# The last mixer step's output handed to the routing front's rounds, and the front's order changed on three engines

## The chip, the cores and the metric

One Trainium2 chip, one of its cores. The metric is the device time of one execution of the whole program, in microseconds (us), of which three were taken for the kernel before.

## What is computed

A block with adaptive layer norm on 8 sequences of 512 tokens and 128 channels: four Mamba-2 layers (`ga` scales what comes out), and then a mixture of experts with one shared expert and 8 routed ones, of which each token takes its best two.

```
h = layernorm(x) * (1 + ca) + sa
for l in range(4):
    h = h + mamba2_layer(rmsnorm(h) * block_norm_w[l], ...)
    # in it: y = rmsnorm(y * silu(z)) * gw; return y @ W_out
x = x + ga * (rmsnorm(h) * final_norm_w)
h = layernorm(x) * (1 + cb) + sb
n = rmsnorm(h) * norm_weight
shared = relu(n @ sw1 + sb1) @ sw2 + sb2
probs = sigmoid(n @ router_w.T); w, idx = normalised top 2 of 8
x = x + gb * (shared + sum of w * expert[idx](n))
```

## The kernel before

Activations lie transposed: 128 channels on the partitions, the 512 tokens of one sequence (a *batch*, n = 0 to 7) in the free dimension. All five engines run hand-ordered lists of instructions with semaphores between them; nothing is scheduled by a tool. There are four stages.

1. *Input.* Load, layer norm, transposes.
2. *Mixer.* 32 steps of one layer and one batch, in a software pipeline of depth three: `body(k)` (L414 and on for TensorE, with a body of its own for each engine) does part A of step k, part B of step k-1 and part C of step k-2. Part C is the end of a layer: `project_out` (two matmuls with W_out, L493 and L494), `square_mean` of the gated output y2 (L479), on ScalarE `square_y`, `log_y`, `root_y` (L1044, L1050, L1055: log and exponential give the reciprocal root), on VectorE `scale_out` (L1484), on GpSimd the sum of the two squares (L1775) and the residual `add_to_h` (L1837). So k = 32 has parts B and C, and k = 33 has part C alone, that of batch 7 in layer 4. Into k = 32 and 33 the first pieces of the front for batch 0 and batch 1 are woven.
3. *Front.* For each batch: square, mean, root of h (`square_h`, `square_mean_of_h`, `root_h`), `add_mamba` (x = x + ga * rmsnorm(h), L1335 and L1338), `mean` and `centre` (L430, L1343), `square_x`, `variance`, `root_x` (L437), `modulate` (L1349, L1351), `square_m`, `square_mean_of_m`, `root_m` (L441, L947, L950), `scale` (L1357), which gives the router's and the experts' input nT. Then `halve` (nT as a sum of two fp32r halves, on ScalarE L955 and on VectorE L1362), `logits` (L446), `exp_logits` (L960), `probability` (L1376), `compare`, `ranks`, `choose` (L1384 to L1401: which two experts), `routing_weight` (L1407 to L1412), `positions` (prefix sums by matmul, L733), `slot` (L1419 to L1424: the row numbers for the scatter). The shared expert goes along: `shared_up(t)` (three matmuls each, L689 to L691, t = 0 to 3), `shared_relu(t)` (L1173), `halves(t)` (L1610, L1612), `shared_down(t)` (L700 to L703), `shared_result` (L1182), `add_shared` (L1618), `turn_base` and `keep_base` (L724, L1195). `turn_tokens` and `put_tokens` (L713, L1190) bring the tokens into rows, and GpSimd scatters them with eight indirect DMAs per batch (L1910) into the experts' slots, after `slot` of that batch.
4. *Experts.* 23 tiles of 512 slots, then the gather and the output.

The order of stage 3 is a function `front(i)` on TensorE, ScalarE and VectorE, called for i = -3 to 10 (`FRONT` is 3); in one round i the pieces belong to batches i-1 to i+3, and a condition drops those outside 0 to 7. The position of a line in `front(i)` is the position in the engine's queue. Before its rounds each of ScalarE and VectorE waits for the whole mixer:

```
steps(dve, body)
dve.wait_ge(hup, NB + STEPS)
```

(`hup` counts the residual sums), followed on VectorE by three set-up operations for the routing.

## Time and profile before

| | us |
|---|---|
| median of three executions | 1090.94 (1088.0 to 1091.41) |
| the profiled execution | 1089.98 |
| its span, first to last instruction | 1088.1 |
| TensorE busy in the span | 948.3 (87%) |
| VectorE busy | 959.5 (88%) |
| ScalarE busy | 846.6 (78%) |
| GpSimd busy | 777.4 (71%) |
| mean granted TensorE clock, share of full speed | 0.961 |

Busy shares are means over four stages. In the trace the mixer's steady part ends near 722 us, its last two bodies reach to about 762, the front's rounds to about 880, and the experts follow from 890. A row of the order of time reads: start, duration, engine, line, operation, output and inputs; in square brackets how long the engine sat idle before it, and what ended that.

### The profile page before, as it was taken

Reading aid. Unit: us, or ns where it says so; the run is one execution under the profiler, and the core shown is the slowest. Engines: PE = TensorE matmul, PEld = TensorE weight load, DVE = VectorE, ACT = ScalarE, POOL = GpSimd, SP = SyncE. Lnnn points to the kernel's source line nnn. Section 1 sums busy time; section 2 is a strip of 40 time slices with the busy share of each in tenths; the row PEclk is TensorE's granted clock in tenths of the full one; section 3 lists DMA queues with packets and bytes.
Section 4 is the critical chain, followed back from the end, with each engine's and each line's share of the span. In section 5 each row is a group of like instructions: output and inputs, shape, how many; then the busy total and the mean of one; then the engine's idle time right before and its main releaser. Section 6 shows DMA issues by size and latency. Waiting matters only on the chain.

```text
span 1088.1 us, 20653 instructions
## 1 busy us (share of the span) xinstructions
PE 948.3 (87%) x6072; PEld 543.3 (50%) x6072; DVE 959.5 (88%) x1769; ACT 846.6 (78%) x1604; POOL 777.4 (71%) x942
## 2 busy tenths in 40 slices
PE   5799999999999999999999999985888759999970
PEld 4344554454445544544554445443455537777750
DVE  6799999999999999999999999975888948888855
ACT  4699999899999998999899989974777625555530
POOL 1289989998998999888877886873355643666660
PEclk9799999999999999999999999998899969999995
DMA  5010232224222322100000000000011136776628
GB/s 151 17 27 13 73 140 71 71 80 152 72 71 85 128 76 86 64 3 3 4 10 2 4 4 4 4 2 1 20 35 35 40 116 190 233 229 224 226 89 231
DMA packets 57422, 83.93 MB, mean 77 GB/s; under 512 B 17562, under 2 KB 37664, under 8 KB 57312
## 3 DMA queue, kind: packets, MB, share of 16 engines
q1 hardware_dynamic: 52320, 74.13, 21.3%
q0 software_dynamic: 4992, 8.48, 2.3%
q8 instruction: 51, 0.84, 0.3%
q14 instruction: 59, 0.48, 0.1%
HBM read 44.99 MB, written 37.83 MB: 76 GB/s over the span
## 4 chain that ended last, share of the span: by engine, by line
PE 28%; ACT 22%; POOL 21%; issue 17%; DVE 8%; DMA 2%; SPq 1%; POOLq 1%; DVEq 0%; ACTq 0%
ACT E L976 3%; POOL dtx L1788 3%; POOL own L1820 3%; PE bank L468 3%; ACT xbc L1081 3%; PE bank L689 2%; POOL yt L1842 2%; PE bank L546 2%; POOL xw L1795 2%; PE bank L703 2%; PE bank L701 2%; PE bank L700 2%; ACT L1070 2%; POOL y L1846 2%; PE bank L690 2%
## 5 line engine op out<-in xcount | busy, mean ns | idle before, releaser
L1449 DVE SCALAR_TENSOR_TENSOR cv<-bank,PAR,cv 128x511 f32<-128x511 f32 (+2 forms) x384 | 276.5, 740 | 6.1 <-ACT cv L988 2.0
L976 ACT ACTIVATE E<-bank 128x512 f32<-128x512 f32 x256 | 144.5, 603 | 44.7 <-PE bank L532 40.1
L1465 DVE SCALAR_TENSOR_TENSOR M<-E,bank 128x512 f32<-128x512 f32 x256 | 170.2, 676 | 1.4 <-ACT E L976 0.4
L1917 POOL DMA_INDIRECT RS<-y,XR x92 | 99.5, 1082 | 78.1 <-DVE y L1697 53.6
L468 PE MATMUL bank<-hn,WA 128*128 128x512 f32 x256 | 142.5, 640 | 3.5 <-DVE cv L1449 3.5
L1842 POOL TENSOR_TENSOR yt<-yt,ti 128x384 f32<-128x384 f32 x64 | 64.1, 1002 | 74.4 <-DVE ti L1522 74.4
L1910 POOL DMA_INDIRECT XS<-stage,IDX x64 | 68.5, 1071 | 56.5 <-DVE run L1424 39.2
L1173 ACT ACTIVATE hr<-bank,W1B 128x512 f32<-128x512 f32 x92 | 63.5, 690 | 56.7 <-PE bank L691 48.9
L1612 DVE TENSOR_TENSOR hL<-hr,hH 128x512 fp32r<-128x512 f32 x124 | 86.9, 701 | 4.3
L1788 POOL TENSOR_TENSOR dtx<-xtok,DTW 128x256 f32<-128x256 f32 x128 | 79.8, 623 | 12.0 <-ACT xtok L996 8.1
L1846 POOL TENSOR_TENSOR y<-yt,zs 128x512 f32<-128x512 f32 x64 | 82.2, 1284 | 5.0
L546 PEld LDWEIGHTS bank<-M,dtx 128*32 128x32 f32 x2048 | 50.9, 109 | 60.5 <-DVE M L1465 32.1
L546 PE MATMUL bank<-M,dtx 128*32 128x128 f32 x2048 | 75.9, 277 | 5.4 <-DVE o_sb L1484 5.4
L1820 POOL TENSOR_TENSOR own<-p,selb 128x512 bf16<-128x512 bf16 x64 | 78.6, 1248 | 0.2 <-PE bank L532 0.2
L1610 DVE CAST hH<-hr 128x512 fp32r<-128x512 f32 x124 | 54.0, 435 | 26.1 <-issue 11.7
L1081 ACT ACTIVATE xbc<-cv 128x512 f32<-128x512 f32 x128 | 73.7, 632 | 0.0
L675 PE MATMUL bank<-hn,WA 128*128 128x512 f32 x128 | 67.5, 649 | 0.0
L1795 POOL TENSOR_TENSOR xw<-xtok,DTW 128x256 f32<-128x256 f32 x96 | 62.5, 651 | 0.0
L510 PEld LDWEIGHTS bank<-CST,xbc 128*128 128x128 f32 x384 | 43.4, 141 | 37.7 <-ACT u L1006 20.3
L996 ACT ACTIVATE xtok<-bank 128x384 f32<-128x384 f32 x128 | 58.1, 481 | 2.5
L510 PE MATMUL bank<-CST,xbc 128*128 128x128 f32 x384 | 54.2, 277 | 5.4 <-ACT u L1006 4.8
L602 PEld LDWEIGHTS bank<-xbc,S 128*128 128x128 f32 x384 | 46.9, 191 | 19.1 <-DVE S L1508 13.8
(239 smaller groups left out, 2586.2 us busy)
## 6 DMA issues: line engine op xcount, KB each, us to landing
XS<-PADT SPq DMA_DIRECT2D x32, 520.0 KB, 4.8
W1B<-WD SPq DMA_DIRECT2D x23, 514.0 KB
W2B<-WD SPq DMA_DIRECT2D x23, 512.5 KB
WD<-WS SPq DMA_DIRECT2D x16, 512.0 KB, 2.9
XR<-XS SPq DMA_DIRECT2D x23, 260.0 KB
RW<-w_in SPq DMA_DIRECT2D x18, 256.0 KB, 4.9
xin<-x_in SPq DMA_DIRECT2D x4, 512.0 KB, 8.5
PC<-p SPq DMA_DIRECT2D x128, 6.0 KB
```

Source lines behind the costliest of these rows:

```text
L468: mm(bank[t % 2][:, :], WA[t][:, :], hn[k % 2][:, :], start=True, stop=True).then_inc(pj_mm, 1)
L510: ins = nc.tensor.transpose(bank[TURN_BANK[c]][:, n * P:(n + 1) * P], conv_rows(t, odd + 1, c * CH, CH), ident)
L546: ins = mm(bank[6 + hh // 4][q:q + 32, c * CH:(c + 1) * CH], dtx[c][:, hh * HD:(hh + 1) * HD], M[2 * (hh // 4) + c % 2][:, (hh % 4) * CH:( ...
L976: f(E[i % 2][:, :], bank[2 + i % 2][:, :], ACT.Exp).then_inc(e_a, 1)
L1081: f(conv_rows(t, odd), cv[t][:, :], ACT.Silu).then_inc(silu_a, 1)
L1449: stt(out=cv[t][:, s:L], in0=src[:, 0:L - s], scalar=PAR[:, bass.ds(cw + 3 - s, 1)], in1=cv[t][:, s:L], op0=ALU.mult, op1=ALU.add).then_in ...
L1465: stt(out=M[i % 4][:, :].rearrange("p (n t) -> p n t", n=4), in0=E[i % 2][:, :].rearrange("p (n t) -> p n t", n=4), scalar=1.0, in1=bank[5 ...
L1612: tt(hL[t][:, :], hr[t][:, :], hH[t][:, :].bitcast(F32), ALU.subtract).then_inc(hl_v, 1)
L1788: tt(dtx[c][:, :].rearrange("p (h d) -> p h d", h=NH), xtok[c][:, 0:DI].rearrange("p (h d) -> p h d", h=NH), DTW[:, 32 * c:32 * c + NH].un ...
L1820: tt(own[:, g * 512:(g + 1) * 512].rearrange("p (h t) -> p h t", h=4), p2[:, :].unsqueeze(1).to_broadcast([P, 4, CH]), selb[:, g * 512:(g ...
L1846: tt(y2[t][:, :], yt[t][:, :], zs[:, bass.ds((j % 2) * 2 * L + t * L, L)], ALU.mult).then_inc(fin_p, 1)
L1917: nc.gpsimd.indirect_dma_start(RS[:, :], bass.IndirectOffsetOnAxis(ap=XR[i % XD][:, (c + 1) * ROW - 1:(c + 1) * ROW].bitcast(I32), axis=0) ...
```

## The change

- `body(33)` is gone on TensorE, ScalarE and VectorE (`steps` ends one k earlier). GpSimd's and SyncE's own loops stay as they are, with k = 33.
- Its work becomes items of the front: TensorE's `last_project_out` and `last_square_mean` in round -3 (now on banks 3 and 4), ScalarE's `last_square_y(0)`, `last_square_y(1)`, `last_log_y` and `last_root_y` in round -2, VectorE's `last_scale_out` in round -3.
- The pieces for batch 1 that were woven into k = 33 come from the rounds: conditions such as `2 <= i + 2` become `1 <= i + 2`.
- The waits for the whole mixer go; narrower ones guard the banks. The three set-up operations move into `choose(0)`.
- The order within `front(i)` is another one on all three engines.

```diff
@@ -227,7 +227,7 @@
 
         def steps(eng, body):
 
-            for k in range(STEPS + 2):
+            for k in range(STEPS + 1):
                 body(k, k % 2, A=k < STEPS, B=1 <= k <= STEPS, C=k >= 2, N=k < STEPS - 1)
...
                 wait(pe, n_v, n + 1)
                 if n == 0:
-                    pe.wait_ge(hup, NB + STEPS)
+                    wait(pe, fin_v, 4 * STEPS)
+                    wait(pe, o_v, STEPS - 1)
...
+            def last_project_out():
+
+                wait(pe, wos_a, 2 * NL)
+                wait(pe, fin_p, 4 * STEPS)
+                wait(pe, fin_v, 4 * STEPS)
+                mm(bank[3][:, :], WO[:, 0:DM], y2[0][:, :], start=True, stop=False)
+                mm(bank[3][:, :], WO[:, DM:2 * DM], y2[1][:, :], start=False, stop=True).then_inc(out_mm, 1)
+
+            def last_square_mean():
+
+                wait(pe, sum_p, STEPS)
+                wait(pe, s_v, 5 * STEPS)
+                wait(pe, e2_a, 2 * STEPS)
+                mm(bank[4][:, :], mean256[:, :], sqy[0][:, :], start=True, stop=True).then_inc(ss_mm, 1)
...
             def front(i):
 
+                if 1 <= i + 1 < NB:
+                    variance(i + 1)
                 if 0 <= i - 1 < NB:
                     turn_base(i - 1)
                 if 0 <= i < NB:
-                    shared_up(i, 0)
-                if 2 <= i + 2 < NB:
-                    mean(i + 2)
-                if 0 <= i < NB:
-                    shared_up(i, 1)
+                    shared_up(i, 2)
                 if 0 <= i < NB:
                     positions(i)
                 if 1 <= i + 1 < NB:
                     square_mean_of_m(i + 1)
                 if 0 <= i < NB:
+                    shared_up(i, 3)
+                if 1 <= i + 2 < NB:
+                    mean(i + 2)
+                if 0 <= i < NB:
                     shared_down(i, 0)
-                if 0 <= i < NB:
-                    shared_up(i, 2)
-                if 0 <= i < NB:
-                    shared_up(i, 3)
+                if i == -3:
+                    last_project_out()
                 if 1 <= i + 1 < NB:
                     logits(i + 1)
-                if 2 <= i + 3 < NB:
-                    square_mean_of_h(i + 3)
                 if 0 <= i + 1 < NB:
                     turn_tokens(i + 1)
                 if 0 <= i < NB:
                     shared_down(i, 1)
+                if 0 <= i + 1 < NB:
+                    shared_up(i + 1, 0)
                 if 0 <= i < NB:
                     shared_down(i, 2)
                 if 0 <= i < NB:
                     shared_down(i, 3)
-                if 1 <= i + 2 < NB:
-                    variance(i + 2)
+                if i == -3:
+                    last_square_mean()
+                if 0 <= i + 1 < NB:
+                    shared_up(i + 1, 1)
+                if 1 <= i + 3 < NB:
+                    square_mean_of_h(i + 3)
...
+            def last_square_y(t):
+
+                wait(act, fin_p, 4 * (STEPS - 1) + 2 + 2 * t)
+                wait(act, ss_mm, STEPS - 1)
+                f(sqy[t][:, :], y2[t][:, :], ACT.Square).then_inc(sq_a, 1)
+
+            def last_log_y():
+
+                wait(act, ss_mm, STEPS)
+                wait(act, o_v, STEPS - 1)
+                f(lnY[:, :], bank[4][:, :], ACT.Ln, bias=eps5).then_inc(ry_a, 1)
+
+            def last_root_y():
+
+                wait(act, ry_a, 2 * STEPS - 1)
+                f(rY[:, :], lnY[:, :], ACT.Exp, scale=-0.5).then_inc(ry_a, 1)
...
             def front(i):
 
+                if i == -2:
+                    last_square_y(0)
+                if 1 <= i + 2 < NB:
+                    root_h(i + 2)
                 if 1 <= i + 1 < NB:
                     root_x(i + 1)
-                if 0 <= i < NB:
-                    shared_relu(i, 0)
                 if 0 <= i - 1 < NB:
                     keep_base(i - 1)
+                if 0 <= i < NB:
+                    shared_relu(i, 1)
+                if 1 <= i + 3 < NB:
+                    square_h(i + 3)
                 if 1 <= i + 1 < NB:
                     square_m(i + 1)
                 if 0 <= i < NB:
-                    shared_relu(i, 1)
+                    shared_relu(i, 2)
                 if 1 <= i + 1 < NB:
                     root_m(i + 1)
-                if 0 <= i < NB:
-                    shared_relu(i, 2)
-                if 2 <= i + 3 < NB:
-                    square_h(i + 3)
+                if 1 <= i + 1 < NB:
+                    halve(i + 1)
+                if i == -2:
+                    last_square_y(1)
+                if 1 <= i + 1 < NB:
+                    exp_logits(i + 1)
+                if i == -2:
+                    last_log_y()
                 if 0 <= i < NB:
                     shared_relu(i, 3)
-                if 1 <= i + 1 < NB:
-                    exp_logits(i + 1)
-                if 2 <= i + 2 < NB:
+                if 0 <= i + 1 < NB:
+                    put_tokens(i + 1)
+                if 0 <= i + 1 < NB:
+                    shared_relu(i + 1, 0)
+                if 1 <= i + 2 < NB:
                     square_x(i + 2)
-                if 2 <= i + 3 < NB:
-                    root_h(i + 3)
-                if 1 <= i + 1 < NB:
-                    halve(i + 1)
                 if 0 <= i < NB:
                     shared_result(i)
-                if 0 <= i + 1 < NB:
-                    put_tokens(i + 1)
+                if i == -2:
+                    last_root_y()
...
             steps(act, body)
-            act.wait_ge(hup, NB + STEPS)
+            wait(act, fin_p, 4 * STEPS - 2)
...
                 wait(dve, rt_v, 20 * n + 7)
                 if n == 0:
+                    stt(out=utb[:, :], in0=CST[:, K_MASK:K_MASK + P], scalar=0.0, in1=ident, op0=ALU.is_ge, op1=ALU.subtract).then_inc(setup_v, 1)
+                    nc.vector.memset(m40[:, :], 0.0).then_inc(setup_v, 1)
+                    dve.wait_ge(iota_p, 3)
+                    cp(run[:, :], first_slot[:, :]).then_inc(setup_v, 1)
                     dve.wait_ge(setup_v, 3)
...
+            def last_scale_out():
+
+                wait(dve, out_mm, STEPS)
+                wait(dve, ry_a, 2 * STEPS)
+                wait(dve, hup, NB + STEPS - 1)
+                tt(o_sb[:, :], bank[3][:, :], rY[:, :], ALU.mult).then_inc(o_v, 1)
...
@@ -1621,36 +1672,38 @@
 
                 if 0 <= i < NB:
                     compare(i)
+                if 0 <= i < NB:
+                    halves(i, 0)
+                if 0 <= i < NB:
+                    ranks(i)
                 if 0 <= i - 1 < NB:
                     add_shared(i - 1)
-                if 1 <= i < NB:
-                    halve(i)
-                if 0 <= i < NB:
-                    ranks(i)
-                if 2 <= i + 2 < NB:
-                    add_mamba(i + 2)
                 if 0 <= i < NB:
                     choose(i)
+                if 1 <= i + 2 < NB:
+                    add_mamba(i + 2)
                 if 1 <= i + 1 < NB:
                     modulate(i + 1)
                 if 0 <= i < NB:
-                    halves(i, 0)
-                if 0 <= i < NB:
                     routing_weight(i)
                 if 0 <= i < NB:
+                    slot(i)
+                if 0 <= i < NB:
                     halves(i, 1)
-                if 2 <= i + 2 < NB:
-                    centre(i + 2)
                 if 1 <= i + 1 < NB:
                     scale(i + 1)
                 if 0 <= i < NB:
-                    slot(i)
-                if 0 <= i < NB:
                     halves(i, 2)
+                if i == -3:
+                    last_scale_out()
+                if 1 <= i + 1 < NB:
+                    halve(i + 1)
                 if 0 <= i < NB:
                     halves(i, 3)
                 if 0 <= i + 1 < NB:
                     probability(i + 1)
+                if 1 <= i + 2 < NB:
+                    centre(i + 2)
...
             steps(dve, body)
-            dve.wait_ge(hup, NB + STEPS)
-            stt(out=utb[:, :], in0=CST[:, K_MASK:K_MASK + P], scalar=0.0, in1=ident, op0=ALU.is_ge, op1=ALU.subtract).then_inc(setup_v, 1)
-            nc.vector.memset(m40[:, :], 0.0).then_inc(setup_v, 1)
-            dve.wait_ge(iota_p, 3)
-            cp(run[:, :], first_slot[:, :]).then_inc(setup_v, 1)
             for i in range(-FRONT, NB + FRONT):
```

Three places of the new order, in a round in the middle of the front. First VectorE, from routing_weight's last row (stage) on; hH and hL are the halves of one relu, nT<-nT,PAR,rf is scale, pos to run are slot, nT<-xT,bank is centre. Before:

```order
L1412 TENSOR_TENSOR stage0<-sw,cs4 128x2x4
L1610 CAST hH1<-hr1 128x512
L1612 TENSOR_TENSOR hL1<-hr1,hH1 128x512
L1343 TENSOR_TENSOR nT0<-xT,bank5 128x512
L1357 SCALAR_TENSOR_TENSOR nT1<-nT1,PAR2,rf1 128x512
L1419 TENSOR_TENSOR pos<-bank7,run 128x32
L1421 TENSOR_TENSOR sel<-oh,pos 128x64
L1422 TENSOR_REDUCE idf<-sel 128x8
L1423 CAST IDX0<-idf 128x8
L1424 TENSOR_TENSOR run<-run,bank7 128x8
```

and now:

```order
L1460 TENSOR_TENSOR stage0<-sw,cs4 128x2x4
L1467 TENSOR_TENSOR pos<-bank7,run 128x32
L1469 TENSOR_TENSOR sel<-oh,pos 128x64
L1470 TENSOR_REDUCE idf<-sel 128x8
L1471 CAST IDX0<-idf 128x8
L1472 TENSOR_TENSOR run<-run,bank7 128x8
L1661 CAST hH1<-hr1 128x512
L1663 TENSOR_TENSOR hL1<-hr1,hH1 128x512
L1401 SCALAR_TENSOR_TENSOR nT1<-nT1,PAR2,rf1 128x512
L1661 CAST hH2<-hr2 128x512
```

Slot stood behind one pair of halves, centre and scale, and now comes straight after routing_weight, ahead of them.

TensorE between the variance (the matmul of sqf1 into bank6) and the square mean of m (the next matmul of sqf1 into bank6, which before stands three rows below what is shown); bank7<-CST,xT is turn_base, the rows with nH and nL are shared_up, those with m40 positions. Before:

```order
L437 MATMUL bank6<-sqf1,mean128 128x512
L724 MATMUL bank7<-CST,xT 128x128 x4
L689 MATMUL bank0<-nH,SW0 128x512
L690 MATMUL bank0<-nH,SW0 128x512
L691 MATMUL bank0<-nL,SW0 128x512
L430 MATMUL bank5<-xT,mean128 128x512
L689 MATMUL bank1<-nH,SW0 128x512
L690 MATMUL bank1<-nH,SW0 128x512
L691 MATMUL bank1<-nL,SW0 128x512
L733 MATMUL bank7<-m40,utb 128x40
L735 MATMUL bank7<-m40,onesb 128x32
L735 MATMUL bank7<-m40,onesb 128x24
```

and now:

```order
L440 MATMUL bank6<-sqf1,mean128 128x512
L724 MATMUL bank7<-CST,xT 128x128 x4
L688 MATMUL bank2<-nH,SW0 128x512
L689 MATMUL bank2<-nH,SW0 128x512
L690 MATMUL bank2<-nL,SW0 128x512
L733 MATMUL bank7<-m40,utb 128x40
L735 MATMUL bank7<-m40,onesb 128x32
L735 MATMUL bank7<-m40,onesb 128x24
L735 MATMUL bank7<-m40,onesb 128x16
L735 MATMUL bank7<-m40,onesb 128x8
L444 MATMUL bank6<-sqf1,mean128 128x512
```

Variance ended a round, and two shared_ups and a mean lay between it and the next square mean; now variance starts the round, and one shared_up and no mean lies between.

ScalarE from the logarithm of root_m (lnf1) to the copy of the tokens (stage) or the result (es); pr is exp_logits, hr3 the relu of t = 3. Before:

```order
L947 ACTIVATE lnf1<-bank6,CST 128x512
L950 ACTIVATE rf1<-lnf1 128x512
L1173 ACTIVATE hr2<-bank2,PAR2 128x512
L908 ACTIVATE sqf0<-h 128x512
L1173 ACTIVATE hr3<-bank3,PAR2 128x512
L960 ACTIVATE pr<-bank6 128x32
L926 ACTIVATE sqf1<-nT0 128x512
L912 ACTIVATE lnf0<-bank5,CST 128x512
L918 ACTIVATE rf0<-lnf0 128x512
L955 ACTIVATE nH<-nT1 128x512
L1182 ACTIVATE es<-bank4,PAR2 128x512
L1190 ACTIVATE stage1<-bank7 128x4x128 x2
```

and now:

```order
L971 ACTIVATE lnf1<-bank6,CST 128x512
L974 ACTIVATE rf1<-lnf1 128x512
L979 ACTIVATE nH<-nT1 128x512
L984 ACTIVATE pr<-bank6 128x32
L1192 ACTIVATE hr3<-bank3,PAR2 128x512
L1209 ACTIVATE stage1<-bank7 128x4x128 x2
L1192 ACTIVATE hr0<-bank0,PAR2 128x512
L950 ACTIVATE sqf1<-nT0 128x512
L1201 ACTIVATE es<-bank4,PAR2 128x512
```

exp_logits stood behind the relu of t = 3 and now stands ahead of it; the relu of t = 0 of the next batch has come forward into this round, behind the tokens.

## Rows read from the trace of the kernel before

**Rows 1.** Stretches, one per round: length, PE PEld DVE ACT POOL busy, clock, DMA

```profile
778.38:793.12 14.74, 11.89 (x55) 7.58 (x54) 13.61 (x37) 10.95 (x20) 8.96 (x10) 1.00 0.13 42
793.12:808.72 15.60, 13.30 (x55) 8.20 (x54) 13.79 (x37) 11.04 (x20) 8.77 (x10) 0.89 0.10 34
823.46:839.09 15.63, 13.33 (x55) 8.20 (x54) 13.77 (x36) 11.03 (x20) 8.78 (x10) 0.89 0.11 35
853.83:866.33 12.50, 10.29 (x50) 6.74 (x48) 11.88 (x33) 8.67 (x15) 8.99 (x10) 1.00 0.13 43
795.00:798.00 3.00, 1.33 (x7) 0.88 (x7) 2.93 (x6) 2.69 (x6) 2.09 (x3) 1.00 0.13 44
798.00:801.00 3.00, 2.57 (x4) 1.45 (x5) 2.93 (x9) 1.10 (x2) 2.39 (x3) 0.56 0.13 44
```

**Rows 2.** VectorE in order of time, second round: start, us, then the instruction

```profile
780.11 0.75 DVE L1618 SCALAR_TENSOR_TENSOR xT<-es,MOD,xT 128x512 f32<-128x512 f32 x1 [0.50 <-ACT es L1182]
...
784.54 0.55 DVE L1351 TENSOR_SCALAR nT<-nT,MOD 128x512 f32<-128x512 f32 x1
785.00 0.42 DVE L1610 CAST hH<-hr 128x512 fp32r<-128x512 f32 x1
...
786.06 0.22 DVE L1407 TENSOR_TENSOR pw<-oh,pm 128x64 f32<-128x64 f32 x1
...
788.13 0.68 DVE L1343 TENSOR_TENSOR nT<-xT,bank 128x512 f32<-128x512 f32 x1
788.73 0.74 DVE L1357 SCALAR_TENSOR_TENSOR nT<-nT,PAR,rf 128x512 f32<-128x512 f32 x1
789.39 0.18 DVE L1419 TENSOR_TENSOR pos<-bank,run 128x32 f32<-128x32 f32 x1
...
790.39 0.43 DVE L1610 CAST hH<-hr 128x512 fp32r<-128x512 f32 x1
...
792.52 0.17 DVE L1376 TENSOR_SCALAR prx<-pr 128x32 f32<-128x32 f32 x1
```

**Rows 3.** TensorE in order of time, second and third round

```profile
785.80 1.12 PE L441 MATMUL bank<-sqf,mean 128*128 128x512 f32 x2 [0.16 <-issue]
...
789.52 1.06 PE L446 MATMUL bank<-PAR,nT 128*128 128x8 f32 x8 [0.52 <-DVE nT L1357]
...
795.93 0.63 PE L724 MATMUL bank<-CST,xT 128*128 128x128 f32 x4 [0.99 <-ACT stage L1190]
...
798.43 2.08 PE L430 MATMUL bank<-xT,mean 128*128 128x512 f32 x2 [1.16 <-DVE xT L1338]
```

**Rows 4.** Chain of waits into the front: start, us, engine and line

```profile
750.51 2.05 PE bank L493 x2
...
755.09 0.70 ACT lnY L1050
...
757.71 1.41 DVE nT L1335
...
761.11 0.70 DVE nT L1343
```

**Rows 5.** In order of time at the front's end: GpSimd, then VectorE

```profile
864.37 1.26 POOL L1910 DMA_INDIRECT XS<-stage,IDX  x1 [1.36 <-DVE run L1424]
...
875.84 1.04 POOL L1910 DMA_INDIRECT XS<-stage,IDX  x1 [0.28 <-issue]
...
874.58 0.17 DVE L1423 CAST IDX<-idf 128x8 int32<-128x8 f32 x1
```

**Rows 6.** ScalarE in order of time, second round

```profile
786.96 0.69 ACT L947 ACTIVATE lnf<-bank,CST 128x512 f32<-128x512 f32 x1 [0.64 <-PE bank L441]
787.68 0.64 ACT L950 ACTIVATE rf<-lnf 128x512 f32<-128x512 f32 x1
...
789.46 0.68 ACT L1173 ACTIVATE hr<-bank,PAR 128x512 f32<-128x512 f32 x1
790.62 0.20 ACT L960 ACTIVATE pr<-bank 128x32 f32<-128x32 f32 x1 [0.48 <-PE bank L446]
```

More of the change, by code:

```diff
@@ L436, in variance @@
                     wait(pe, s1_v, 3)
+                elif n == 1:
+                    wait(pe, fin_v, 4 * STEPS)
+                    wait(pe, ry_a, 2 * STEPS - 2)
                 mm(second_bank(n)[:, :], mean128[:, :], sqf[own_set(n)][:, :], start=True, stop=True).then_inc(var_mm, 1)
@@ L625, in body @@
                     square_mean()
-                if C and not B:
-                    square_mean_of_h(1)
                 if B:
@@ L631, in body @@
                     project(3)
-                if C and not B:
-                    mean(1)
                 if B and not A:
@@ L736, in positions @@
                 ins.then_inc(pos_mm, 1)
+            def last_project_out():
+                wait(pe, wos_a, 2 * NL)
+                wait(pe, fin_p, 4 * STEPS)
+                wait(pe, fin_v, 4 * STEPS)
+                mm(bank[3][:, :], WO[:, 0:DM], y2[0][:, :], start=True, stop=False)
[5 more added lines that the diff above has]
+                mm(bank[4][:, :], mean256[:, :], sqy[0][:, :], start=True, stop=True).then_inc(ss_mm, 1)
             def shared_up(n, t):
@@ L746, in shared_up @@
                         wait(pe, ex_a, 1)
+                        wait(pe, fin_v, 4 * STEPS)
+                if n == 0 and t == 3:
+                    wait(pe, o_v, STEPS)
                 up(n, t, SW[0], nH[:, half], nL[:, half])
             def shared_down(n, t):
+                if n == 0 and t == 0:
+                    wait(pe, ry_a, 2 * STEPS - 1)
                 down(n, t, SW[1])
             def front(i):
+                if 1 <= i + 1 < NB:
+                    variance(i + 1)
                 if 0 <= i - 1 < NB:
@@ L1111, in body @@
                     norm_root(k + 1)
-                if C and not B:
-                    square_h(1)
                 if A:
@@ L1127, in body @@
                     tap(3)
-                if C and not B:
-                    root_h(1)
-                    square_x(1)
                 if B and not A:
@@ L1553, in body @@
                     scale_out()
-                if C and not B:
-                    add_mamba(1)
                 if A:
                     tap(2, 3)
-                if C and not B:
-                    centre(1)
                 if B and not A:
```

## The prediction

> **What bounds the kernel now.** I read the table of stretches first, one stretch per round of the routing front, from one compare to the next [rows 1]. A round takes 14.74 us with TensorE's clock at 1.00 and VectorE busy for 13.61 of it; no other engine passes 12. So VectorE sets the round. In VectorE's own order of time the only wait of such a round is 0.50 us before add_shared (L1618) [rows 2]. The third round takes 15.60 us at a mean clock of 0.89; the fifth reads 15.63, so two of the five full rounds (the two between and the last stand as the second, 14.74) cost 0.86 us more. Ahead of the third round's fall TensorE had 1.33 us of work in 795 to 798, and in 798 to 801 the mean clock is 0.56 [rows 1]: it went from the 2.4 GHz level to the 1.2 GHz level after turn_base and one shared_up between two waits [rows 3].
>
> The way into the front is in the chain of waits [rows 4]. The last step's projection starts at 750.51, its square mean is done when ScalarE takes the logarithm at 755.09, then come root_h(1), add_mamba(1) at 757.71 and centre(1) at 761.11. This is one serial chain over four engines; what surrounds it is idle.
>
> The way out: VectorE finishes the last slot numbers at 874.75, GpSimd issues the last eight scatters from 875.84, having waited 0.28 us since its previous eight [rows 5]. The experts need all of them landed. One batch of scatters holds GpSimd 864.37 to 875.84, 11.5 us, so it has slack in a round of 14.7 but hardly any at the end. **What counts is when slot(7) is ready on VectorE.**
>
> **The head: no gain.** The change lifts project_out, square_mean, log and root, scale_out out of the body for k = 33 and gives them to rounds -3 and -2. But VectorE's round -3 holds only last_scale_out, which waits for last_root_y, and that stands behind the same y2, the same two projections and the same square mean in the same order on TensorE. add_mamba(1) still comes behind it. I keep 757.71 for add_mamba(1) and 761.11 for centre(1). The removed table load of k = 33 lies in a wait for y2 and is worth nothing; if that cover went, it would have been paid before too. The three set-up operations move behind ranks(0), so compare(0) starts at 761.7 and not at 762.6. Then halves(0,0) comes second in the round: it waits for turn_tokens(0), the first shared_up, put_tokens(0) and one relu, which I estimate to start only after mean(1) ends, just before 761.11, and to take 2.9 us at the low clock, so 764.0, some 1.15 us after compare(0) is through. GpSimd and SyncE run the same list as before; they lose and gain no issue.
>
> **The round at full clock.** All lists hold the same work per round, so I lay VectorE's new order out from compare(i) = 0 with start-to-start steps of [rows 2]. Before, modulate's second half (L1351) starts 784.54 - 778.38 = 6.16 after compare. Now the 0.50 wait goes (the result is taken a round later), halve (0.60, as the centre step 788.13 to 788.73) goes behind it, halves(i,0) (785.00 to 786.06, 1.06) comes ahead: 6.12. From there:
> - scale needs square, square mean, log and root first. L1351 to TensorE's square mean is 785.80 - 784.54 = 1.26, to the log 1.16 more, log and root 1.40 [rows 3, 6]: 3.82, so scale can start at 9.94. VectorE is there at 6.12 + 0.46 + 1.01 (routing_weight: 786.06 to 788.13 less a halves) + 1.00 (slot) + 1.06 (halves 1) = 9.65. It waits 0.29.
> - scale 0.66, halves 2 1.06, halve 0.60: 12.26. halves 3 needs relu 3, which ScalarE now has behind exp_logits. Logits start 0.79 after scale's start, exp_logits 1.10 later (789.52, 790.62), then 0.1 and a relu of 0.68 [rows 3, 6]: 9.94 + 0.79 + 1.10 + 0.10 + 0.68 = 12.61. It waits 0.35.
> - halves 3 1.06, probability 0.60, centre 0.60: **14.87 us**. The one wait of 0.50 has become two of 0.64 together. At full clock the round gains nothing.
>
> **The clock.** In the new list of TensorE, variance(i+1) is followed by turn_base, one shared_up, positions, and then square_mean_of_m(i+1). The first of these waits for add_shared, at about 3.7 in the round; the last one for square_m, at about 7.25. variance ends at about 2.7: 4.6 us with turn_base and shared_up (1.33 as in 795 to 798) and 0.2 of positions as all its work. Before, the same 1.33 us lay between shorter waits (0.99 and 1.16) and the clock fell in two of five rounds. I estimate four of five now. In the low stretch square_mean_of_m, shared_up 3, mean, shared_down 0 and logits stand one behind the other, and logits releases exp_logits and so relu 3. That string is 789.52 - 785.80 = 3.72 us before [rows 3]; the low stretch before cost TensorE 13.30 - 11.89 = 1.4 us of work [rows 1]. If it falls wholly into the string, the round is 14.87 + 1.4 = 16.3; if half, 15.6. I take 1.25 per fall, **15.87 us** for a mean round. Here a rule speaks for the change and against me. The Trainium skill, "TensorE: Matmul & The Clock Gate", section "HAM oscillation — how this bites in real kernels", puts the danger in one unbroken idle gap of TensorE longer than any in either order; by it no round would fall. This trace does not agree: the fall near 798 came with no unbroken wait above 1.16 us [rows 3]. By the page the sum would be that of the first rival.
>
> **The sum.**
> - compare(1), against 778.38: at full clock 761.7 + 14.87 + 1.15 + 0.3 for the set-up = 778.0, with a likely fall (0.85 x 1.25) 779.1: +0.7.
> - compare(1) to compare(6), five rounds: 79.35 against 853.83 - 778.38 = 75.45: +3.9.
> - Round 6 lacks add_mamba and centre (about 2.0). By the chain of scale and logits I get 12.7 at full clock, 13.3 with falls, against 12.50 [rows 1]: +0.8.
> - compare(7) to slot(7) done: before 874.75 - 866.33 = 8.42. Now halves 1 stands behind slot, and slot waits for positions, which needs add_shared, turn_base and keep_base: 6.0. -2.4.
> - GpSimd's start behind it: -0.1, since its previous eight are then done in time (slot(6) + 1.0 + 11.5 is before it).
> Together +2.9. VectorE's tile map and TensorE's gate matmuls end some 1.4 us later after slot(7) than before, behind halves 1 to 3; the landing of the last scatters and the first load of slots hide them, and I cost them at nothing (1 us were that cover gone). The 23 expert tiles and the end are unchanged. Against the profiled execution's 1089.98 this gives **1092.9 us**; that execution lay 1 us under the median of the three, 1090.94. A measurement of this kernel tells some 0.3% from no change, 3.3 us.
>
> **Rivals.**
> - *The clock holds.* The longer quiet stretch does not lower it. Then compare(1) -0.4, five rounds 74.35 (-1.1), round 6 +0.2, -2.5 at the end: -3.8, and the idle of the set-up may overlap a little more: **1085.8 us**. For it: 1.33 us between waits passed without a fall in three of five rounds. Against: the stretch is a third longer. This is also what the page would give.
> - *TensorE at half clock decides every round.* The fall meets the string square mean to logits each time: 16.35 a round, +6.3; compare(1) +0.8, round 6 +1.1, end -2.5: +5.7, **1095.7 us**, slower. It decides once the fall comes before or within that string in nearly all rounds. For it: the head of the string follows the quiet stretch directly. Against: some falls end before logits.
> - *The head is shortened after all,* which the words of the change promise, by ScalarE's and TensorE's items filling the waits. The chain of [rows 4] leaves no place; were square_mean_of_h(1) to go first, root_h(1) would still stand behind last_root_y. Worth at most 0.5 us; I count it within the others.
>
> **How the numbers follow.** Forecast (falls in most rounds, little net) 0.42, own range 1088.5 to 1094. The clock holds 0.28. Half clock decides 0.30; part of the forecast's upper end counts as slower, part of this rival's lower end as no change. The unknown of 0.3 us a round in my waits is 2 us either way over the front. The range 1085 to 1097 leaves out less than 2 in 10.
>
> **What would show it.** In the changed profile: add_mamba(1) near 757.7; the first scatter near 772.3; rounds of 15.5 to 16.3 with a low clock behind square_m, VectorE waiting before scale and before halves 3 for ScalarE's relu behind exp_logits; slot(7) near 877.7, the last scatters from 878.6. I am wrong if rounds read 14.9 or less at full clock (first rival), or if VectorE's wait lies elsewhere, as before modulate.

## The result and the profile after

The changed kernel takes 1097.82 us in the median of 20 executions (1090.49 to 1104.37), the kernel before 1090.96 us (1086.77 to 1093.3, also 20). The ratio is 1.006, 95% interval 1.0046 to 1.0074: **slower, by 5 to 8 us**, which is beyond the forecast of 1092.9 and 0.8 us outside its range (1085 to 1097). The profiled execution took 1096.32, 6.3 more than that of before (1089.98). Executions over 1.5% slower than the fastest of their kernel (two of e2, one of e10) are left out of every figure below. The scatter is a result as well: 14 us where it was 6.5. Over the 20 executions time and clock go together: the two fastest (1090.49) had a mean clock of 0.960 and 0.959 over the whole span, the slowest (1104.37) 0.944.

First the same stretches as in [rows 1], from compare to compare, rounds 1 to 6 of the changed kernel (length, then busy time of PE, PEld, DVE, ACT, POOL, then PEclk, DMA share, GB/s):

```profile
782.32:796.94 14.62, 11.75 (x55) 7.67 (x54) 13.55 (x38) 10.95 (x19) 7.56 (x8) 1.00 0.10 33
796.94:812.94 16.00, 13.12 (x55) 8.60 (x54) 13.55 (x37) 10.96 (x19) 9.95 (x10) 0.89 0.12 38
812.94:827.56 14.62, 11.74 (x55) 7.69 (x54) 13.55 (x37) 10.96 (x19) 7.57 (x8) 1.00 0.11 34
827.56:843.79 16.23, 13.36 (x56) 8.81 (x55) 13.77 (x38) 10.96 (x19) 10.18 (x10) 0.89 0.12 38
843.79:860.70 16.91, 13.80 (x54) 8.79 (x53) 13.68 (x37) 10.51 (x18) 9.36 (x10) 0.80 0.11 35
860.70:874.78 14.08, 11.10 (x49) 7.26 (x48) 11.73 (x34) 9.09 (x16) 7.67 (x9) 0.88 0.11 35
```

At clock 1.00 a round takes 14.62, a shade less than the 14.74 of before. The three others of the five full ones take 16.00, 16.23 and 16.91, with the clock at 0.89, 0.89 and 0.80; before, a round with a fall took 15.60 or 15.63. VectorE works 13.55 to 13.77 us in all of them.

TensorE in order of time in round 2 (to be set beside [rows 3]); variance is L440, turn_base L724, the shared_ups end with L690, positions L733, square_mean_of_m L444, mean L430, logits L449:

```profile
798.69 1.02 PE L440 MATMUL bank<-sqf,mean 128*128 128x512 f32 x2
800.72 0.66 PE L724 MATMUL bank<-CST,xT 128*128 128x128 f32 x4 [1.01 <-DVE xT L1669]
...
801.67 0.40 PE L690 MATMUL bank<-nL,SW 128*128 128x512 f32 x1
802.15 0.18 PE L733 MATMUL bank<-m,utb 128*128 128x40 bf16 x1
...
804.21 1.17 PE L444 MATMUL bank<-sqf,mean 128*128 128x512 f32 x2 [1.79 <-ACT sqf L966]
...
805.60 0.63 PE L689 MATMUL bank<-nH,SW 128*128 128x512 f32 x1
806.03 0.63 PE L690 MATMUL bank<-nL,SW 128*128 128x512 f32 x1
806.46 1.91 PE L430 MATMUL bank<-xT,mean 128*128 128x512 f32 x2
...
809.05 0.95 PE L449 MATMUL bank<-PAR,nT 128*128 128x8 f32 x8
```

This is the quiet stretch of the forecast: from the end of variance at 799.7 to 804.2, 4.5 us, TensorE has turn_base, one shared_up and positions, 1.6 us of work. Behind it the matmuls of the shared_up take 0.63 and not 0.40, mean takes 1.91 and not 1.02: the low clock (0.50 from 805.2 to 808.5) lies in the string from the square mean to logits. Rounds 1 and 3 have the same stretch with the same waits, and the clock stays at 1.00; so the stretch makes a fall possible, and what decides between these rounds is not seen in these rows. VectorE's waits in the same round, and ScalarE's:

```profile
806.80 0.75 DVE L1401 SCALAR_TENSOR_TENSOR nT<-nT,PAR,rf 128x512 f32<-128x512 f32 x1 [0.24 <-ACT rf L974]
...
810.85 0.43 DVE L1661 CAST hH<-hr 128x512 fp32r<-128x512 f32 x1 [1.63 <-ACT hr L1192]
```

```profile
810.04 0.20 ACT L984 ACTIVATE pr<-bank 128x32 f32<-128x32 f32 x1 [1.82 <-PE bank L449]
810.13 0.68 ACT L1192 ACTIVATE hr<-bank,PAR 128x512 f32<-128x512 f32 x1
```

ScalarE waits 1.82 us for logits, and only then does the relu for which VectorE has waited 1.63. At full clock the same two waits are short (round 3):

```profile
822.76 0.75 DVE L1401 SCALAR_TENSOR_TENSOR nT<-nT,PAR,rf 128x512 f32<-128x512 f32 x1 [0.19 <-ACT rf L974]
...
825.47 0.43 DVE L1661 CAST hH<-hr 128x512 fp32r<-128x512 f32 x1 [0.29 <-ACT hr L1192]
```

The way in is as it was, a chain over four engines (as [rows 4]; ahead of what is shown GpSimd makes y2):

```profile
752.51 2.05 PE bank L743 x2
...
757.77 0.70 ACT lnY L1226
...
760.39 1.41 DVE nT L1379
...
762.57 2.07 PE bank L430 x2
```

And the way out (as [rows 5]), GpSimd at the head of the last eight scatters, behind VectorE's last slot numbers:

```profile
882.09 1.26 POOL L1958 DMA_INDIRECT XS<-stage,IDX  x1 [2.57 <-DVE run L1472]
```

```profile
880.31 0.19 DVE L1467 TENSOR_TENSOR pos<-bank,run 128x32 f32<-128x32 f32 x1 [0.40 <-PE bank L735]
...
881.05 0.17 DVE L1471 CAST IDX<-idf 128x8 int32<-128x8 f32 x1
```

GpSimd had been idle for 2.57 us, so its own scatters do not set the end; slot(7) does, 6.5 us later than before (881.22 against 874.75). From there to the end the two profiles agree within 0.3 us: low_slots(0) starts at 892.6 of 1088.1 before, at 899.15 of 1094.5 now.

### The profile page after: what moved, and what is told of

Read it like the earlier page. It is cut to its first block, busy times and chain, and to the rows that moved or that the text cites. A ratio compares the mean times of both kernels' runs of the same rounds, so it can differ in the third digit from the quotient of the medians.

```text
span 1094.5 us, 20653 instructions
## 1 busy us (share of the span) xinstructions
PE 954.9 (87%) x6072; PEld 549.9 (50%) x6072; DVE 960.4 (88%) x1769; ACT 844.7 (77%) x1603; POOL 774.8 (71%) x942
## 4 chain that ended last, share of the span: by engine, by line
PE 26%; ACT 18%; issue 9%; DVE 9%; POOL 2%; DMA 1%; SPq 0%; ACTq 0%; POOLq 0%; DVEq 0%
PE bank L688 3%; ACT E L1000 3%; PE bank L689 2%; PE bank L690 2%; ACT xbc L1105 2%; PE bank L699 2%; PE bank L700 2%; PE bank L702 2%; PE bank L549 2%; PE bank L471 2%; ACT L1094 2%; ACT xtok L1020 2%; PE bank L430 1%; ACT sqy L1068 1%; DVE o_sb L1532 1%
```

## The experiments

Every ratio is to the kernel before, timed with it on the same chip, with its 95% interval. A difference between two experiments is one of medians from different chips, on which the kernel before has 1090.4 to 1091.3. Besides the time each profile gives the lengths of rounds. Names: e1 and so on.

### e1, the moved work alone

`front(i)` has the order of before on all three engines; body 33 is gone and its items stand in rounds -3 and -2, and set-up in `choose(0)`. On TensorE, against the changed kernel:

```diff
-                if 1 <= i + 1 < NB:
-                    variance(i + 1)
                 if 0 <= i - 1 < NB:
                     turn_base(i - 1)
                 if 0 <= i < NB:
-                    shared_up(i, 2)
+                    shared_up(i, 0)
+                if 1 <= i + 2 < NB:
+                    mean(i + 2)
+                if 0 <= i < NB:
+                    shared_up(i, 1)
...
```

> The moved work alone: body 33 gone and its items in the rounds, but every front(i) in the order of before. Theory A (the loss sits in the new order, through TensorE's clock): as before, ratio 0.998 to 1.002, rounds from compare to compare of 14.7 us at full clock and 15.6 where the clock falls, compare(0) some 0.5 us earlier behind centre(1). Rival B (the head costs: what follows k = 32 got longer): ratio 1.003 or more, with scale_out or add_mamba(1) late by 2 us or more against the end of the last y2.

Measured: 0.9987 (0.9971 to 1.0003), 1091.29 us. Rounds of 14.73 at clock 1.00, and 15.54 and 15.65 at 0.89. Its profile has the same late head as the changed kernel's (scale_out at 759.50; the changed kernel 759.21, the kernel before 756.52), and still the kernel is not slower in the median. Most of the lateness is there before any changed code runs. The scale_out ahead of the last one, in the kernel before and in the changed kernel:

```profile
734.42 0.69 DVE L1484 TENSOR_TENSOR o_sb<-bank,rY 128x512 f32<-128x512 f32 x1 [2.02 <-ACT rY L1055]
```

```profile
736.47 0.69 DVE L1532 TENSOR_TENSOR o_sb<-bank,rY 128x512 f32<-128x512 f32 x1 [3.33 <-ACT rY L1079]
```

In the stretch ahead of it the clock was low for 3.4 us in the one profile (from 726.7) and twice as long in the other. In the profiles of e3, e4, e6 and e7, which have the changed kernel's head as it is, this row stands at 731.9 to 733.8 and compare(0) at 762.20, 761.48, 759.20 and 759.29, against 765.29. So some 2 us of the 6.3 between the two first profiles are where the low clock fell in that execution, and not the change. The moved head costs nothing, and by its interval gains 3 us at most.

### e2, the new order alone

Body 33 stays with the pieces of batch 1, `front(i)` has the new order; against the changed kernel:

```diff
-            for k in range(STEPS + 1):
+            for k in range(STEPS + 2):
...
-                if 1 <= i + 2 < NB:
+                if 2 <= i + 2 < NB:
                     mean(i + 2)
...
```

> The new order alone: body 33 stays with the pieces of batch 1 woven in, and only front(i) has the new order. Theory A: most or all of the loss, ratio 1.004 to 1.008, rounds of 14.6 at full clock and 16.0 to 16.9 with a fall, falls in about 3 of 5 rounds. Rival B: ratio below 1.002.

Measured: 1.0046 (1.0019 to 1.0072), 1098.55 us, 1087.84 to 1100.17. All of the loss that the runs can tell from nothing is here (the changed kernel has 1.006, and e1 none). Its rounds 1 to 5:

```profile
780.55:797.90 17.35, 14.48 (x56) 9.31 (x55) 13.89 (x37) 10.95 (x19) 9.50 (x11) 0.80 0.10 35
797.90:815.36 17.46, 13.49 (x54) 8.65 (x53) 13.87 (x37) 10.93 (x19) 8.07 (x9) 0.80 0.09 31
815.36:832.28 16.92, 13.14 (x55) 8.52 (x54) 13.64 (x37) 10.82 (x19) 8.10 (x9) 0.90 0.10 30
832.28:846.90 14.62, 11.74 (x55) 7.67 (x54) 13.55 (x37) 10.96 (x19) 7.57 (x8) 1.00 0.10 32
846.90:862.92 16.02, 13.12 (x55) 8.56 (x54) 13.55 (x37) 10.45 (x18) 9.97 (x10) 0.89 0.11 37
```

One round in five keeps the clock and takes 14.62. The first two stand at 0.80 over 17.4 us: the clock was low for 7 us of the round, twice as long as in the last one (0.89, 16.02). The third (0.90, 16.92) has a low stretch no longer than the last one's and is still late: in it TensorE waits 1.49 us ahead of positions, where a round at full clock has no wait.

### e3, the relu of t = 3 put forward

```diff
+                if 0 <= i < NB:
+                    shared_relu(i, 3)
                 if 1 <= i + 1 < NB:
                     exp_logits(i + 1)
                 if i == -2:
                     last_log_y()
-                if 0 <= i < NB:
-                    shared_relu(i, 3)
```

> The changed kernel with the relu of t = 3 ahead of exp_logits on ScalarE. Theory A: the wait before halves 3 is only where a late logits shows; with the relu in front it goes (0.3 us in a round at full clock, 1.5 to 1.7 in one with a fall), but what logits releases behind it (probability, compare) is then late by some of it: 2 to 4 us of the 7 come back, ratio to before 1.002 to 1.004. Rival C (the order of these two is all of the loss): ratio 1.000 or below. Rival D (it doesn't matter, the next wait takes it all): ratio 1.006.

Measured: 1.0026 (1.0007 to 1.0046), 1093.54 us: 4 of the 7 us come back. A round at full clock is now 14.23, VectorE with no wait before halves 3; but one with a long low stretch is still 17.87:

```profile
792.85:807.08 14.23, 11.73 (x55) 7.67 (x54) 13.45 (x37) 11.03 (x20) 9.44 (x10) 1.00 0.12 38
821.51:839.38 17.87, 13.81 (x56) 9.10 (x55) 13.81 (x38) 11.26 (x20) 9.11 (x10) 0.81 0.10 34
```

So the order of these two on ScalarE is a part, and the clock is left. Part of a fall shows a round later: round 1 of this profile takes 15.23 at clock 1.00, behind a round 0 at 0.82.

### e4, extra matmuls in the two waits of a round

The changed kernel, with work for TensorE where it waits. The results are overwritten by the shared_up that follows; nothing of the computation is left out.

```diff
+            def fill(i, b, count):
+                ...
+                wait(pe, r_a, HT * (i - 1) + b + 1)
+                for _ in range(count):
+                    mm(bank[b][:, :], SW[0][:, 0:P], nH[:, half], start=True, stop=True)
...
                     variance(i + 1)
+                if 0 <= i < NB:
+                    fill(i, 2, 4)
...
                     positions(i)
+                if 0 <= i < NB - 1:
+                    fill(i, 3, 7)
```

> The changed kernel with eleven extra matmuls a round on TensorE, 512 columns each, into banks that are free there: four behind variance, seven behind positions, which fill its two waits and whose results are overwritten (nothing of the computation is left out). Theory A (clock): no fall in rounds 1 to 5, clock 1.00, every round 14.6 us; the time drops by 5 to 8 us against the changed kernel and scatters less from run to run, ratio to before 0.997 to 1.001. If the clock is not the cause, rounds stay at their lengths, or get longer by the extra 2.5 us of TensorE work, and the ratio is 1.006 or more.

Measured: 0.9971 (0.9955 to 0.9987), 1088.31 us, 1085.28 to 1091.29. **Eleven useless matmuls a round take 9.5 us off the changed kernel** and make it faster than the one before. All full rounds are 14.62 to 14.64 at clock 1.00, with TensorE 14.1 to 14.4 us busy, as this one:

```profile
791.90:806.53 14.63, 14.20 (x66) 9.60 (x65) 13.56 (x37) 11.04 (x19) 8.88 (x9) 1.00 0.11 37
```

TensorE in the stretch; L780 is the extra work (rows of the same line merged):

```profile
793.65 1.02 PE L440 MATMUL bank<-sqf,mean 128*128 128x512 f32 x2
794.10 1.48 PE L780 MATMUL bank<-nH,SW 128*128 128x512 f32 x4
795.68 0.65 PE L724 MATMUL bank<-CST,xT 128*128 128x128 f32 x4
...
797.36 0.18 PE L733 MATMUL bank<-m,utb 128*128 128x40 bf16 x1 [0.33 <-issue]
...
797.49 1.87 PE L780 MATMUL bank<-nH,SW 128*128 128x512 f32 x7
799.19 1.11 PE L444 MATMUL bank<-sqf,mean 128*128 128x512 f32 x2
```

### e5, the same for the kernel before

Four extra matmuls ahead of turn_base and five ahead of mean, in the old order.

```diff
+                if 0 < i < NB:
+                    fill(i, 0, 4)
                 if 0 <= i - 1 < NB:
                     turn_base(i - 1)
                 if 0 <= i < NB:
                     shared_up(i, 0)
+                if 0 <= i < NB:
+                    fill(i, 1, 5)
                 if 2 <= i + 2 < NB:
                     mean(i + 2)
```

> The kernel before with nine extra matmuls a round in TensorE's two waits (four ahead of turn_base, five ahead of mean), results overwritten, nothing left out. Theory A: its falls go too, every full round 14.7 us; it had falls in 2 of 5 rounds at 0.9 us and one in its first, so 1.5 to 3 us come back, ratio to before 0.997 to 0.999. If only the new order had a clock problem: ratio 1.000.

Measured: 0.9987 (0.9970 to 1.0004), 1089.62 us. Its five rounds take 73.65 us at clock 1.00, 14.73 each, against 75.45 before. The gain is of the expected size, and too small for its interval to exclude none.

### e6, half of the extra matmuls

The seven behind positions alone:

```diff
                     variance(i + 1)
-                if 0 <= i < NB:
-                    fill(i, 2, 4)
```

> The changed kernel with the seven extra matmuls behind positions alone, none behind variance. Theory A, in which the quiet stretch as a whole counts: the seven nearly double TensorE's work in it, so most falls go and the time lies near that with eleven, ratio to before 0.997 to 1.000. If each wait counts by itself (the wait behind variance, 1.0 us, is left as it is): falls stay in some rounds, ratio 1.002 or more.

Measured: 0.9978 (0.9965 to 0.9992), 1088.59 us, no different from eleven. From compare(1) to compare(5):

```profile
774.97:833.45 58.48, 53.86 (x242) 35.31 (x241) 54.19 (x145) 43.83 (x76) 35.52 (x36) 1.00 0.12 38
```

Four rounds of 14.62 at clock 1.00, with the wait behind variance (1.0 us) left as it was. It is not each wait by itself that lowers the clock. Nor is it likely to be the longest one, the 1.79 that was filled here: in the kernel before the clock fell near 798.4 behind waits of 0.99 and 1.16 [rows 3], and at 747.1, 0.4 us into a wait, behind waits of 0.74, 0.51 and 1.04, while e6 keeps 1.01 and 1.03 in its rounds without a fall. No run varies the work and the waits apart.

### e7, both edits of e3 and e4

The two diffs above together.

> The changed kernel with the relu of t = 3 ahead of exp_logits and the eleven extra matmuls. Theory A: at full clock this order's round is 14.2 us (read in the run with the relu alone), against 14.6 with the extra matmuls alone and 14.7 of before: another 2 to 2.5 us over the rounds, ratio to before 0.994 to 0.996. Rival: with a string this tight the extra TensorE work shows, rounds of 14.6 or more, ratio 0.997.

Measured: 0.9947 (0.9926 to 0.9968), 1084.7 us. Rounds of 14.24 or 14.25 at clock 1.00, in which VectorE waits once, for 0.20 us.

### e8, e9 and e10: the waits ahead of the front

```diff
+            def burn(dst, count):
+                wait(pe, split_p, 4)
+                for _ in range(count):
+                    mm(dst[:, :], SW[0][:, 0:P], SW[0][:, 0:512], start=True, stop=True)
...
                 if B and not A:
+                    wait(pe, s1_a, 2)
+                    burn(bank[0], 8)
                     mean(0)
...
             def last_project_out():
                 wait(pe, wos_a, 2 * NL)
+                wait(pe, fin_v, 4 * STEPS)
+                burn(bank[3], 8)
                 wait(pe, fin_p, 4 * STEPS)
-                wait(pe, fin_v, 4 * STEPS)
...
+                if i == -1:
+                    wait(pe, ex_a, 1)
+                    burn(bank[0], 10)
                 if 1 <= i + 2 < NB:
                     mean(i + 2)
```

e8 adds this to e7.

> The same, with extra matmuls also in the three waits ahead of the front: 8 ahead of mean(0), 8 while y2 is being made, 10 ahead of mean(1). Theory A: the projection, square mean and mean that ran at half clock there (2.05, 1.9, 1.7 and 2.1 us in the changed kernel's profile, 1.0 each at full clock) lose some 3 to 5 us in the chain into the front; ratio to before 0.990 to 0.993. If those waits are longer than the extra work bridges, the clock falls all the same and the ratio is that of the run without them.

Measured: 0.9909 (0.9887 to 0.9931), 1081.18 us in four executions, 1080.38 to 1081.74. The chain of [rows 4] in e8, L457 being the extra work:

```profile
746.29 2.06 PE L457 MATMUL bank<-SW 128*128 128x512 f32 x8 [0.78 <-issue]
749.23 1.12 PE L752 MATMUL bank<-y,WO 128*128 128x512 f32 x2 [0.88 <-POOL y L1919]
750.20 1.02 PE L753 MATMUL bank<-y,WO 128*128 128x512 f32 x2
751.24 1.12 PE L760 MATMUL bank<-sqy,mean 128*128 128x512 f32 x2
752.20 1.02 PE L425 MATMUL bank<-sqf,mean 128*128 128x512 f32 x2
...
757.22 1.12 PE L430 MATMUL bank<-xT,mean 128*128 128x512 f32 x2 [1.70 <-DVE xT L1407]
```

The two projections take 1.12 and 1.02 where the changed kernel's profile has 2.05 and 1.9, mean(1) 1.12 and not 2.07.

e9 has all the extra work in the kernel before (in k = 33 into bank 7).

> The kernel before with extra matmuls in its rounds and in the same three waits ahead of the front (8, 8, 10). It tells what the new order would be worth if the clock held in both. Theory A: against the run with extra matmuls in the rounds alone 2 to 4 us come back, ratio to before 0.995 to 0.997, so the changed order with its relu put forward, held at full clock, is 4 to 5 us better than the old order held at full clock. Rival: the old order gains as much as the new one (0.991), and order is worth nothing.

Measured: 0.9958 (0.9940 to 0.9975), 1085.7 us. Its profile still had a fall, in round 0 (16.14 us at clock 0.79), and behind it a round of 15.61 at clock 1.00. With extra work in both, the new order with its relu put forward is 4.5 us better than the old one (1081.18 against 1085.7; the two were not timed side by side, and their ratios to before, 0.9909 and 0.9958, differ by 5 us). Not all of that is the order: e8's profile has no fall in these rounds. In rounds 2 to 5, at clock 1.00 in both, the new order takes 14.24 and the old one 14.74, 0.5 us a round.

e10 has it in the changed kernel, ahead of the front alone.

> The changed kernel with extra matmuls only in the three waits ahead of the front, none in the rounds. Theory A: 2 to 4 us less than the changed kernel, rounds still 16 to 17 us where the clock falls: ratio to before 1.002 to 1.005. If the head's low clock were the larger part of the loss: ratio 1.000 or below.

Measured: 1.0053 (1.0022 to 1.0085), 1095.34 us, 1085.15 to 1100.75. It gives back 2.5 us in the medians and less than 1 by the ratios, whose intervals overlap, and the wide scatter stays: the larger part of the loss is in the rounds. Its profiled execution is the fastest of its twelve (three of five rounds at 14.6, the others 16.0).

### e11 and e12: the stretch filled with work of its own

Instead of extra matmuls two pieces move into the quiet stretch; the relu is put forward as in e3.

```diff
                     variance(i + 1)
+                if 0 <= i < NB:
+                    shared_up(i, 1)
...
                     positions(i)
+                if 1 <= i + 2 < NB:
+                    mean(i + 2)
...
                     shared_up(i, 3)
-                if 1 <= i + 2 < NB:
-                    mean(i + 2)
...
-                if 0 <= i + 1 < NB:
-                    shared_up(i + 1, 1)
```

> The changed kernel with the relu of t = 3 put forward and, in place of extra matmuls, two pieces of TensorE's own work moved into its quiet stretch: shared_up(i,1) behind variance, mean(i+2) behind positions. No work is added or left out. Theory A: the stretch of 4.6 us then holds about 3.2 us of work and not 1.5, and the string from the square mean to logits is 0.9 us shorter; falls become rare, rounds 14.2 to 14.4 us, ratio to before 0.995 to 0.998. If the string alone mattered and not the clock: falls go on, 15 us a round, 1.000.

Measured: 0.9920 (0.9900 to 0.9941), 1083.31 us, 1080.06 to 1085.26. Rounds 1 to 5 are 14.23 or 14.24 each, at clock 1.00, with no matmul more than before; one of them:

```profile
792.85:807.09 14.24, 11.97 (x55) 7.60 (x54) 13.46 (x38) 11.17 (x20) 9.46 (x10) 1.00 0.12 38
```

```profile
796.63 0.66 PE L724 MATMUL bank<-CST,xT 128*128 128x128 f32 x4 [0.63 <-DVE xT L1669]
...
798.27 1.12 PE L430 MATMUL bank<-xT,mean 128*128 128x512 f32 x2
800.11 1.12 PE L444 MATMUL bank<-sqf,mean 128*128 128x512 f32 x2 [0.72 <-ACT sqf L966]
...
803.47 1.06 PE L449 MATMUL bank<-PAR,nT 128*128 128x8 f32 x8 [0.85 <-DVE nT L1401]
```

TensorE's waits are now 0.63, 0.72 and 0.85, and none of 1.79. Against e3, which has the relu put forward alone, the two moves bring 10 us. They shorten the string behind the square mean by the mean as well, so not all of it need be the clock.

e12 is e11 with the extra matmuls ahead of the front.

> The same, with the extra matmuls in the three waits ahead of the front (8, 8, 10), where there is no work of its own to move in. Theory A: 3 to 4 us less again, ratio to before 0.991 to 0.994, near the 0.991 of the kernel with extra matmuls everywhere.

Measured: 0.9900 (0.9880 to 0.9920), 1079.25 us, 1078.45 to 1083.06. **The fastest version, 11.7 us faster than the kernel before and 18.6 than the changed one**, by the medians; from e8 (0.9909) and e11 (0.9920) its interval doesn't separate it.

## Why the prediction was wrong

Point by point, against the profile of the changed kernel:

- *What bounds it; the head: no gain.* Right. VectorE sets a round at full clock; the chain into the front is the same (e1: 0.9987); the table load that is gone, 1.28 us at 746.21 in the old trace, stood in a wait. The 0.9 us of the set-up came as forecast where mean(1) kept its clock: from scale_out to compare(0) 5.13 us in e6 and e7, 6.07 before.
- *The round at full clock.* Forecast 14.87, two waits of 0.29 and 0.35 in place of one of 0.50. Measured 14.62, with waits of 0.19 and 0.29 at just these places. The order is exact, the length 0.25 too long: 0.16 of that is the two waits; the rest was not traced.
- *The clock falls in most rounds.* Right in kind: 3 of 5 in this profile, 4 of 5 in that of e2; forecast 4 of 5. The rule of the Trainium skill, "TensorE: Matmul & The Clock Gate", section "HAM oscillation — how this bites in real kernels", names an unbroken idle gap longer than any wait of these rounds as what lowers the clock, and so spoke against it. The runs show that keeping to the rule is not enough: in the full rounds of the changed kernel no unbroken wait is above 1.79 us, and the clock fell all the same. With work put into the stretch it fell in none of the full rounds (e4, e6).
- *What a fall costs.* **This is the step that failed.** I took 1.25 us a fall, from one low stretch of the old trace (1.4 us of lost work), and 16.35 us as the longest round (14.87 + 1.4 is 16.27). Measured over the round at full clock: 1.38, 1.61 and 2.29 here, 2.73, 2.84, 2.30 and 1.40 in e2, on average 2.1 (the two falls of e10's profile, its fastest execution, 1.39 each). So the shortest cost is already the whole of the lost work, and the clock was low for up to twice as long in one round (0.80 over 17 us), which my bound did not contain. No round of the old trace shows such a stretch, but its head does, and I did not use it: low from 747.1 to 754.0 and from 760.8 to 767.7, 7 us each. In round 5 of the changed kernel the fall comes at 849.5, while TensorE still waits, and the clock stays low without a break to 856.3; square_mean_of_m itself then runs at half clock (2.07 us and not 1.1), and the string behind comes late as a whole:

```profile
851.05 2.07 PE L444 MATMUL bank<-sqf,mean 128*128 128x512 f32 x2 [1.79 <-ACT sqf L966]
...
854.20 1.91 PE L430 MATMUL bank<-xT,mean 128*128 128x512 f32 x2
...
856.81 0.95 PE L449 MATMUL bank<-PAR,nT 128*128 128x8 f32 x8
```

- *The sum.* Rounds 1 to 5: forecast 79.35, measured 78.38 here and 82.37 in e2, 80.4 on average. The round at full clock, 0.25 too long, hid 1.2 us of the dearer falls; that was luck. Round 6: 13.3 forecast, 14.08 measured in both. compare(7) to slot(7): 6.0 against 6.44. compare(0) to compare(1), forecast 17.4: 17.03 and 16.31. So in the changed kernel's own profile the rounds are 1 us under the forecast, and its 3.4 us over 1092.9 stand ahead of compare(0), 765.29 where I had 761.7: 2.0 of them are the lateness from before the changed code (e1), the rest is the low clock over the square mean and mean(1). That the dear falls are what the median shows rests on e2 and e4.
- *The rivals.* The second, half clock decides, named the mechanism and the direction, at 1095.7; I gave it 0.30 and the milder case 0.42. The probable size of a fall decided between them. The first rival, the clock holds, would have given 1085.8; e4, where it is made to hold in the rounds and not ahead of them, measured 1088.3. The third gave nothing, as forecast.
- *What would show it.* The first scatter at 775.64 (forecast 772.3, the head was late), slot(7) at 881.2 (877.7), VectorE's waits where they were named.

What stays open: the medians of the changed kernel and of e2 lie 7 us over before, while the terms of the profiles make some 5 (rounds 80.4 - 75.45 = 4.9, round 6 +1.6, the end -2.0, round 0 +0.9). The intervals of the ratios (5 to 8 us, 2 to 8 us) hold both. One profile is one execution out of a scatter of 14 us, and the other executions have no profile. Open too is what decides whether a quiet stretch ends in a fall.

## What to carry to other kernels

Lay out a new order at both clocks: how much work TensorE has in its quietest stretch, and which string stands behind it. Here a stretch of 4.5 us with 1.6 us of work in it cost 2 us in most rounds, though no single wait was above 1.79; seven spare matmuls kept the clock up in the rounds and made the kernel 9 us faster, and so did two pieces of its own work moved in, with one relu put forward (14 us, of which the relu alone brings 4). And when bounding such a cost, don't take the one instance in the old trace as its size: the order that provokes it also gets more of it.

## What was not expected of the hardware

- Extra matmuls of 512 columns, 0.23 us each, whose results nobody uses, speed this kernel up: 1097.8 to 1088.3 with eleven a round (e4), and to 1088.6 with seven (e6).
- The scatter between executions goes with the clock: 14 us in the changed kernel, between 0.944 and 0.961; 6 us in twelve executions of e4, between 0.962 and 0.967; 1.4 us in e8, of which there are only four.
- The time lost to a fall can be more than TensorE's own extra work: in e2's round of 17.46 us at clock 0.80 TensorE is busy 13.49 and not 11.74, 1.75 more, and the round is 2.84 longer than at full clock. In its round of 16.02 at 0.89 both are 1.4.
